# The second mixture of 14 experts: its norm, logits, routing and sending taken out of its own stage and written into the causal attention loop and among the expert tiles

## The reference, cut to what matters

```python
x = x + 0.5 * _L1_ffn_ref(_layernorm(x), gate_w, w1, b1, w2, b2)     # mixture of 14, first time
x = x + _L1_attn_ref(_layernorm(x), W_qkv, b_qkv, W_out, b_out)      # causal attention, 16 heads of 64
x = x + 0.5 * _L1_ffn_ref(_layernorm(x), gate_w, w1, b1, w2, b2)     # mixture of 14, second time
```

```python
probs = softmax(h @ gate_w.T)                  # 14 experts
top2_p, top2_i = top_k(probs, 2)
w = top2_p / max(sum(top2_p), 1e-10)
y_e = gelu(h @ w1[e] + b1[e]) @ w2[e] + b2[e]  # only the two chosen experts are needed
result = clip(h + w[0] * y_e0 + w[1] * y_e1, -100, 100)
```

## Time and profile before

| | |
|---|---|
| median of 3 runs | 4322.61 us (4318.81 to 4332.14) |
| the profiled execution's own time | 4312.76 us |
| its span, first to last instruction | 4310.6 us |
| mean granted TensorE clock | 0.923 |
| causal stage: loop of 32 iterations | 2945 to 3976 us of the span |
| second `ffn1`, first half (preamble) | 3979.5 to 4044.4 us |
| second `ffn1`, second half (tiles) | 4044.4 to 4310.6 us |
| busy, whole span | PE 85%, DVE 73%, ACT 46%, POOL 28% |

### The profile page before, as it was taken

One profiled execution on the slowest core, in us unless ns is written; L12 is line 12 of the kernel. 1 busy time (PEld: TensorE's weight loads), 2 busy tenths in 40 slices (PEclk: granted clock), 3 DMA queues, 4 the chain that ended last, 5 costly groups with the idle time before them and its releaser, 6 DMA issues. The chain is left out here.

```text
span 4310.6 us, 59958 instructions
## 1 busy us (share of the span) xinstructions
PE 3664.0 (85%) x20847; PEld 1626.9 (38%) x20847; DVE 3126.4 (73%) x7330; ACT 2000.5 (46%) x2982; POOL 1187.6 (28%) x1186
## 2 busy tenths in 40 slices
PE   6999999889789789999997874548999999998464
PEld 2222222254344422222224444544444444443464
DVE  7999999366666799999974664356767767765434
ACT  2677777521344337777773112323444444443132
POOL 1000000010312100000000114434666666666533
PEclk8999999999899879999998986778999999999587
DMA  4111111200300041111112012330000000000233
GB/s 119 56 54 52 49 52 50 91 25 1 105 1 1 24 106 49 52 52 54 53 38 100 1 46 73 87 90 2 2 2 2 2 2 2 2 2 17 83 100 93
DMA packets 326956, 192.82 MB, mean 45 GB/s; under 512 B 168606, under 2 KB 282066, under 8 KB 326658
## 3 DMA queue, kind: packets, MB, share of 16 engines
q1 hardware_dynamic: 310594, 155.14, 13.4%
q0 software_dynamic: 14336, 33.58, 2.7%
q10 hardware_dynamic: 1728, 0.28, 0.0%
HBM read 119.74 MB, written 67.90 MB: 44 GB/s over the span
## 5 line engine op out<-in xcount | busy, mean ns | idle before, releaser
L774 DVE TENSOR_REDUCE ra_mh<-PS 128x1 f32<-128x512 f32 x2048 | 1300.1, 683 | 21.3 <-PE PS L640 9.6
L722 ACT ACTIVATE ra_p<-PS 128x1024 f32<-128x1024 f32 x1024 | 994.2, 1021 | 436.4 <-PE PS L648 436.0
L657 PE MATMUL PS<-ra_p,ra_va 128*32 128x512 f32 x4096 | 563.8, 605 | 0.3
L648 PE MATMUL PS<-ra_q,ra_k 75*128 75x512 bf16 x2048 | 537.2, 383 | 3.8 <-ACT ra_p L722 1.5
L610 POOL DMA_DIRECT2D o_heads<-rp_rot x128 | 67.4, 531 | 1482.7 <-ACT rp_rot L730 1482.7
L2336 ACT ACTIVATE ca_p<-PS 128x1024 f32<-128x1024 f32 (+3 forms) x384 | 304.8, 811 | 357.9 <-PE PS L2235 355.9
L2386 POOL TENSOR_TENSOR ca_s<-ca_s,ca_p 128x1024 f32<-128x1024 f32 (+3 forms) x256 | 412.3, 1611 | 75.4 <-ACT ca_p L2336 54.8
L640 PE MATMUL PS<-ra_ko,ra_qo 48*128 48x512 bf16 x1024 | 408.0, 398 | 24.1 <-DVE ra_mh L774 24.1
L640 PE MATMUL PS<-ra_k,ra_q 48*128 48x512 bf16 x1024 | 407.1, 398 | 16.6 <-DMA ra_qo<-q_parts 16.0
L640 PEld LDWEIGHTS PS<-ra_k,ra_q 48*128 48x128 bf16 x1024 | 94.9, 93 | 656.0 <-DVE ra_mh L774 537.4
L2231 PE MATMUL PS<-ca_q,ca_k 64*128 64x512 f32 (+3 forms) x1536 | 318.5, 495 | 0.0
(11 more groups left out here) (261 smaller groups left out, 5582.2 us busy)
## 6 DMA issues: line engine op xcount, KB each, us to landing
ra_k<-k_parts SPq DMA_DIRECT2D x128, 144.0 KB
ra_q<-q_parts SPq DMA_DIRECT2D x128, 144.0 KB
o_heads<-rp_rot POOLq DMA_DIRECT2D x128, 128.0 KB
ao_ot<-o_heads SPq DMA_DIRECT2D x16, 1024.0 KB
f_xg<-expert_tokens SPq DMA_DIRECT2D x56, 256.0 KB, 3.3
expert_outputs<-f_yb SPq DMA_DIRECT2D x56, 256.0 KB, 2.1
expert_tokens<-X SPq DMA_DIRECT2D x28, 256.0 KB, 3.7
q_parts<-rp_parts SPq DMA_DIRECT2D x48, 128.0 KB, 2.4
```

Of the source, the lines that this page charges most:

```text
L648: mm = pe.matmul(PS[:, j, :], K[0:KROWS, ub, j, (step % KT) * P:(step % KT + 1) * P], Q[0:KROWS, ub, j, (step // KT) * BT:(step // KT + 1) ...
L657: mm = pe.matmul(PS[VW * j:VW * (j + 1), 4, :], VA[:, ub, step % KT, j, :], PR[:, s % 2, j, :], start=(s % KT == 0), stop=(s % KT == KT - ...
L722: act.activation(PR[:, s % 2, PH * pair:PH * (pair + 1), :], PS[:, PH * pair:PH * (pair + 1), :], ACT.Exp, scale=float(DH) ** -0.5).then_i ...
L774: dve.tensor_reduce(mh[:, pair, KT * odd + t, h:h + 1], PS[:, bank, :], AX.X, ALU.max).then_inc(s_max, 1)
```

## The change

The first mixture keeps its function, renamed `ffn1_alone`. For the second one a class `Front` holds norm, logits, routing and sending, each as a method for one engine, and two places call them.

- `causal` hosts batches 0, 1 and 2 (`HOSTED = 3`). All loads of gate, constants and weights are issued in the preamble of the causal stage. Counting iterations k from the end of a batch (k = n - 8(b + 1)): DVE takes the statistics at k = 0 and 1, POOL makes the reciprocal roots at k = 1, DVE norms at k = 1 and 2, PE turns at k = 2 (two fills of the ring, `x`), makes logits at k = 3 (`l`) and ranks at k = 6 (`r`); ACT reads these banks and takes the exponentials at the end of k = 3. DVE routes in nine parts at k = 3 to 7, each behind part 2 of pair 1 or of pair 4. POOL sends at k = 8 to 11: three in the skipped step (1, 0), one before step (1, 2). For batch 2 these iterations do not exist; its sends open the last stage.
- `ffn1` starts with tiles at once. Batch 3 is normed and routed among the first 22 pairs of tiles, on a spare bank (7) of PSUM; the results of `down` have two banks where they had three. POOL's order is send 2, fetch 0, send 3, fetch 1, 2, 3.
- The routing reads its logits and ranks from SBUF, where ACT has copied them, no longer from PSUM. It handles each batch by itself, with 112 columns.

```diff
-        causal(nc, a, g)
-        clear_semaphores(nc)
-        ffn1(nc, a, g, out)
+        with ExitStack() as held:
+            front = Front(a, g, *stage(nc, held, FRONT))
+            causal(nc, a, g, front)
+            clear_semaphores(nc)
+            ffn1(nc, a, g, front, 3, 2, dict(x=6, l=3, r=3), out)
...
+    def send(self, pool, b, i):
+        n, k = KT * b + i // 2, i % 2
+        if i == 0:
+            pool.wait_ge(self.s_slot, b + 1)
+        pool.indirect_dma_start(self.g["GT"][b], bass.IndirectOffsetOnAxis(self.slot[:, k, n:n + 1], 0),
+                                self.g["XN"][:, n, :], None).then_inc(self.s_sc[b], 16)
...
+    HOSTED = 3
+    FILL = {(2, 1): ("x", 0), (2, 4): ("x", 1), (3, 1): ("l", 0), (6, 1): ("r", 0)}
...
                 sp.dma_start(wo[:, :, :], a["L1_attn_W_out"].rearrange("(p c) f -> c p f", p=NP)).then_inc(s_w, 16)
+                front.sync(sp)
...
+                        if early and k == 1:
+                            for m in range(HALVES * b, HALVES * (b + 1)):
+                                front.rstd(pool, m)
+                        if NP <= k < NP + 4:
+                            for i in range(4 * (k - NP), 4 * (k - NP) + 3) if early else (4 * (k - NP) + 3,):
+                                front.send(pool, b, i)
...
                         if (qc, kt) == (1, 0):
+                            hosted(n, True)
                             continue
+                        if (qc, kt) == (1, 2):
+                            hosted(n, False)
...
+                ROUTED = ((3, 1), (4, 0), (4, 1), (5, 0), (5, 1), (6, 1), (7, 0), (7, 1))
...
+                            if (pair, part) in ((1, 2), (4, 1)):
+                                hosted(n, pair // 4)
...
-    UB, YB, WB, YR = 3, 3, 8, 4
+    UB, YB, WB, YR = 3, 2, 8, 4
...
+    ORDER = [("send", 2), ("fetch", 0), ("send", 3), ("fetch", 1), ("fetch", 2), ("fetch", 3)]
+    BEGIN = {b: 1 + 8 * (b - hosted) for b in range(hosted, BATCH)}
+    FILL, READ, EXPS, NORM, PART = {"x": (4, 6), "l": (8,), "r": (16,)}, {"x": (5, 7), "l": (10,), "r": (18,)}, 12, 2, (
+        10, 12, 13, 14, 15, 18, 19, 20, 21)
```

520 lines of the change are left out of this document (510 added, 10 removed).

## The result

| | before | changed |
|---|---|---|
| median of 4 runs | 4321.91 us (4318.81 to 4332.14) | 4261.06 us (4257.36 to 4268.07) |
| profiled execution, own time | 4312.76 us | 4257.36 us |
| its span, mean granted clock | 4310.6 us, 0.923 | 4255.5 us, 0.931 |

The ratio is 0.986, with an interval of 0.9848 to 0.9873: 61 us faster, where 46 were forecast (4273 us) and the range was 4240 to 4316.

The account below looks back on a forecast made before the run. PE bounds the causal loop; the last stage is preamble, tiles and POOL's DMA runs, hardly overlapped. 78 us gained there less 32 paid in the loop (12 + 10 + 10) is 46 faster: from 4319 to 4273 us, range 4240 to 4316.

Parts of the forecast that it names:

- rival 1: Causal loop: short sends do not touch PE; only 16 us paid, 62 us faster, 4257 us; chance 0.17.
- The last stage: Stage after the causal loop: shrinks from 331 to about 253 us, net 78 us gained (70 to 90).
- the 83 reckoned for the start and POOL's run: Last stage's start: first turn after 5 us instead of 65, 16 sends ahead, 14 tiles at 33 us: gain 83 us.
- The 5 us for batch 3's routing: Last stage, first 22 pairs of tiles: norm and routing of batch 3 cost 5 us, bounds 0 to 14.
- the second bank of `down` in place of a third: Last stage: one bank fewer for `down` costs nothing, as DVE empties a pair in 0.5 us.
- PE in the loop, 12: Causal loop: three batches' matmuls cost 9.4 us at full price, plus gaps for banks: +12 us, bounds 9 and 20.
- DVE in the loop, 10: Causal loop: routing portions mostly fit DVE's idle time; last portion sticks out 1.4 us a batch; +10 us, 4 to 48.
- rival 2: Causal loop: DVE becomes second bound, routing waits for POOL's sums, 48 us instead of 10; 4311 us; chance 0.13.
- POOL in the loop, 10: Causal loop: 32 sends, each group of three charged 1.2 us, plus what roots add: +10 us, 0 to 40.
- rival 3: Last stage: tiles run straight into sends and fetches, second half ends only 40 us earlier; 4311 us; chance 0.06.
- Rival 4: Causal loop: sends hold PE beyond their end, 118 us instead of 10; 62 us slower, 4381 us; chance 0.06.
- the marks set: Profile signs: PE above 93% busy, routing iterations about 1 us longer, sending ones 1 to 2; over 3 refutes.

## Why the prediction was right, and where its terms were off

**The whole.** The two profiled executions differ by 55.1 us: 77.9 gained in the last stage, 22.7 paid ahead of it. So the stage came out as forecast, 78, and what is paid came to 22.7 instead of 32. The other 6 of the 61 us are not a term of the sum; they come from how far each profiled execution lies from its median, which the forecast had said it could not tell. The measured 4261 is nearer to rival 1's 4257 than to the forecast's 4273, and in the loop the mechanism is rival 1's too, to which I gave 0.17.

**The last stage.** 331 to about 253 us: it is 253.2. The first turn came at 4004.9, 3 us after the barrier's first load, where 5 were allowed. The part up to fetch 0 shrank by 80 us, with the 83 reckoned for the start and POOL's run; 14 tiles were done at 35 us, forecast for 33. What held these tiles was what the text took from the earlier trace rows: POOL's indirect DMAs in a row, on this kind of chip. "From there both versions" run nearly alike: 165.8 us from fetch 0 to fetch 3 now, 161.6 before. The 5 us for batch 3's routing cannot be read alone. From fetch 0 to fetch 1, where most of the routing stands, it is 68.1 us now and 69.2 before, so beside the hold nothing of it shows. On the chip without the hold this stretch takes 40.2 us and the ones after it 31.2 and 31.0, so there it costs up to 9, inside the bounds of 0 to 14. What is longer on this chip is the stretch from fetch 2 to fetch 3, 48.3 against 43.5, behind the routing. Whether the second bank of `down` in place of a third, which I costed at nothing, has to do with it was not tested.

**PE in the loop, 12.** Measured 3.9 us a batch, 11.6, if the whole of the ranks' interval is PE's. The group lengths halved at full clock as reckoned: one turn 0.60, logits 1.85 us, ranks 0.5. Together the matmuls are 10.6 us, where 9.4 were reckoned. The gaps for banks did not appear one by one; all together they are about 1 us.

**DVE in the loop, 10.** Measured 1.8 us a batch, 5.5 in all. The last portion stuck out by 1.2, forecast 1.4; the picks by 0.6; the rest not at all. The Trainium skill's rule (SBUF — State Buffer, Who interferes with whom) on operations with two SBUF inputs beside a GpSimd instruction that reads SBUF agrees with f_o, f_wt and f_big in the changed kernel's loop (f_slot's cast has one such input and is the case of the earlier trace rows). Mean ns stands after the bar's first number:

```profile
L2113 DVE TENSOR_TENSOR f_o<-f_rc,f_ix 128x112 f32<-128x112 f32 x6 | 5.5, 916 | 0.2
L2137 DVE TENSOR_TENSOR f_wt<-f_m,f_gr 128x8 f32<-128x8 f32 x3 | 4.3, 1420 | 0.1
L2157 DVE CAST f_slot<-f_df 128x16 uint32<-128x16 f32 x3 | 4.1, 1366 | 0.1
L2142 DVE TENSOR_TENSOR f_big<-f_rk,f_rc 128x112 f32<-128x112 f32 x3 | 2.8, 929 | 0.0
```

The mean of f_o mixes two cases, three of each. Of the first pick, beside a sum of POOL, and of the second, with POOL idle:

```profile
3365.88 1.81 POOL L2974 TENSOR_TENSOR ca_s<-ca_s,ca_p 128x768 f32<-128x768 f32 x1
3366.26 1.56 DVE L2113 TENSOR_TENSOR f_o<-f_rc,f_ix 128x112 f32<-128x112 f32 x1
...
3380.84 0.27 DVE L2113 TENSOR_TENSOR f_o<-f_rc,f_ix 128x112 f32<-128x112 f32 x1
```

The first ends 0.13 us behind the sum, as if it had waited for all of it; f_wt, a product of 8 columns, takes 1.42 us and ends 0.02 us behind one. So the operations of rival 2 were indeed up to 1.3 us late. What the rival had wrong is that each of them meets a sum, and that this reaches PE: DVE's idle time took it, to the last bit at the picks, as the run with doubled picks shows.

**POOL in the loop, 10.** This is the term that was oversized: 32 sends cost 0.7 to 4 us, under 1 in half of the executions. The 2 us of lateness behind the roots was right, and so was that it need not cost; I charged each group of three 1.2 us because of one late addition in the earlier trace rows, which stood in a run that went on. Rival 1, with 16 us for the loop, was right in this part, and PE and DVE by themselves are about its sum: 11.6 and 5.5 for 16. Of the 22.7 us by which the stage starts later, 17 are these terms, some 3.5 the sends and the one disturbed interval of that execution (its iterations 2 to 30 sum to 956.8), 0.7 the first interval, and 1.7 lies ahead of the loop.

**The rivals.** DVE as a second bound (rival 2) did not decide, but there is no room left at the picks. The smaller gain behind the loop (rival 3) did not come: the stage is 78 us shorter, not 40. Rival 4, sends holding PE beyond their end, is excluded by these 0.7 to 4 us, and by the 14 tiles at 35 us. Of the marks set, PE's share of over 93% is met with 96.7%; iterations that route are 0.1 to 2.1 us longer. Of two iterations with sends beside the roots the first is about 2 us longer than without sends and the next 0.4 to 1.7 shorter; the longest against the same place before is iteration 24 with 2.8, just inside the 3 us that would have spoken against the forecast.

**What the forecast could not see.** Its 78 us holds for chips on which the hold exists. The change by itself was not run on one of the others. An estimate: there before needs 217 us less, of which 110 in the first mixture, so 107 in the last stage, which is then about 224 us (227 by the 263.8 us of before's own trace in that mixture); the kernels that contain the change need 177.9 to 178.5 us for it. That is 46 less in the stage and 22 more in the loop, some 24 us faster, 27 by the other figure. The runs there of the kernels nearest to the change agree with it: 25 us for the all-paced one, 31 for direct sends.

## What to carry to other kernels

Long runs of indirect DMAs from POOL beside a PE-bound stretch are to be broken up: one or two per step of the other engines, with a wait on their progress. Here it gave back 55 us on top of the change on a chip with the hold. On a chip without it the last stage takes about the same paced (178.5 us) as with direct sends and runs of fetches (177.9), and pacing the first mixture cost 9 us. A loop bound by PE takes work on other engines almost free until an engine's idle time at that very place is used up, and then pays at least one for one; so ask which portion stands at which step, not what share is idle. And before a stage's time is explained, look at the same instructions on another chip.

## What the hardware showed that was not expected

- Two kinds of chips: before takes 4322 to 4325 us on some and 4104.5 to 4104.7 on others, with the same instructions, clock 0.92 against 0.943. Where one kernel was traced on both (direct sends), 156 of 159 us of the difference lie in the two mixtures, in which POOL issues indirect DMAs in runs; on the slower kind PE does 80 matmuls beside 32 of them, on the faster over 300. The Trainium skill (SBUF — State Buffer, Who interferes with whom) states that PE and ACT never wait on anyone; the faster kind agrees with it, the slower does not, though no run tells whether the wait is one for SBUF, of which the page speaks.
- On the slower kind the hold needs a run. Groups of three indirect DMAs in the loop (0.7 to 4 us for 32) and single ones between pairs (32.8 and 30.3 us a stretch instead of 49.4 and 48.3) left PE nearly alone on the slower kind too.
- Ordinary DMAs issued by POOL take 0.65 us each on average, and 13 in a row (4020.42 to 4028.85) hold nothing: the first stretch takes 47.6 us with them on both kinds of chip.

```profile
4020.42 8.43 POOL L2191 DMA_DIRECT2D expert_tokens<-XN  x13
```
